# A sixteen-sequence fused layer with a hand-written order on five engines: the order of the steps is rewritten

## Chip, cores, metric

One core of one Trainium2 chip runs one program. The metric is the device time of one execution in microseconds (us), the median of several executions. TensorE (PE) multiplies, VectorE (DVE), ScalarE (ACT) and GpSimd (POOL) work element by element, SyncE (SP) issues the transfers (DMA). Each engine takes its instructions strictly in the order of its own list, and semaphores tie the lists together.

## What is computed

The input is 16 sequences of 375 rows and 128 features. Each sequence goes through three stages, and no sequence needs another one, except that the router's counts run on from one to the next.

```python
# token mixer: two-tap convolution, three gates, a scan over the rows
z, f, o = tanh(conv(x, W_z)), sigmoid(conv(x, W_f)), sigmoid(conv(x, W_o))
c = f * c + (1 - f) * z;  h = o * c
# attention over 39 fixed distances (0 to 32, 48, 64, 96, 128, 192, 256), 8 heads
q, k, v = layernorm(h) @ W_qkv
attn = softmax over the distances of (q . k[n - distance] / 4 + bias)
h = h + (attn . v[n - distance]) * sigmoid(layernorm(h) @ W_gate) @ W_out
# feed-forward with a top-2 router over 64 experts of capacity 128, one shared pair of weights
h = h + (gate of the experts that still had room) * (gelu(layernorm(h) @ w1.T) @ w2.T)
```

## The kernel before

One sequence is a chain of some 40 steps, each a small function of the program (`convolve`, `turn_x`, `project`, `score`, `turn_band`, `attend`, `up`, `down` on PE; `gelu`, `softmax_dense`, `tanh_gate` and so on on ACT). A step waits on the semaphores of the steps that it reads from and of the step that last used its buffer, issues one to 48 instructions, and adds one to its own semaphore.

The sequences are pipelined by hand. On each engine a function `turn(at)` lists the steps of one turn; `at(n)` is the sequence n places behind the newest one, and up to seven sequences are in work at once. `pipeline(engine, turn, range(...))` unrolls the turns. The first turns and the last ones are written out step by step, as lists of their own. So the order of work is nothing but the order of these lines, five times over, and an engine never takes a step ahead of one that waits.

In the text, s is the sequence whose 39 scores PE sums in the turn at hand. In the same turn s+1 is normed and projected to q, k, v and gate, s+3 and s+4 are convolved, s-1 has its attention band turned (`turn_band`), its values summed (`attend`), is turned (`turn_o`) and projected (`out_project`), and s-2 goes through the router and the feed-forward (`turn_x2`, four `up` blocks, `logits`, `positions`, `down`).

ACT uses two sets of function tables: one for tanh and gelu (called TANH in the program), one for exp and ln (LOG). The helper `table` emits a load when a step asks for the set that is not in place; copies and additions ask for none. The table in place is known only from the order of the list:

```python
            def table(name):
                if loaded[0] != name:
                    act.preload_act_table_set(name)
                    loaded[0] = name
```

The steps on ACT that matter below are: `norm2_back` (L925, copies the turned rows of s-2 for the feed-forward), `softmax_dense` (L934, exp of the 33 near scores), `softmax_far` (L941), `softmax_exp` (L950, exp of all scores), `tanh_o` (L819), `gelu` (L972), `logit_copy` (L956), `router_exp` (L965) and `tanh_gate` (L872). A table load has L799.

PE's results stand in eight PSUM banks, and each kind of result has a fixed one (`HOME`). A PE step that reuses a bank names the last users, and waits until they are read. `out_project` of s-1 (L505) shares bank 0 with the first `up` block of s-2 (L529), so it waits for `gelu(s-2, 0)`; `down` (L552) waits for gelu blocks 1 and 2.

The products of q and k are made in eight blocks of near distances and the far ones: POOL makes three of the eight and all far ones (L1724, L1709), DVE the other five (L1247). POOL's first block for a sequence waits for its q and k; `tanh_gate` of s+1 frees the bank in which the scores of s+1 begin.

Of the kernel before, what the change touches and what calls it, by code (L numbers as in the profile page):

```python
# [77 lines left out]
def build(nc, x, params, out):  # L78
# [5 lines left out]
    with ExitStack() as ctx:  # L84
# [12 lines left out]
        def P(name, a=0, b=None):  # L97
            lo, hi = COL[name]
            if lo >= PCOLS:
# [38 lines left out]
        lg = sb("lg", [128, TT, EXPERTS + 8])  # L138
# [19 lines left out]
        HOME = dict(z=4, f=1, o=7, ht=2, xb=0, q=3, k=7, v=1, g=5, s0=4, s2=5, s1=5, ts0=4, ts1=3, ts2=5, tb0=1,  # L158
                    tb1=0, tb2=6, pv=1, ot=1, op=0, x2b=4, lg=6, pos=7, up0=0, up1=5, up2=7, up3=4, dn=6)
# [99 lines left out]
        def _(sp):  # L259
# [78 lines left out]
            def turn(at):  # L338
                a0, a3, a4, a6 = at(0), at(3), at(4), at(6)
                if a4:  # L340
                    read_far(a4)
                if a0 and not (isinstance(a0.b, int) and a0.b < 3):
                    load_x(a0)
                if a4:
                    write_attn(a4)
                    read_values(a4)
                    read_band(a4)
                if a3:
                    write_values(a3)
                    read_near(a3)  # L350
                if a6:
                    store_out(a6)

            load_x(seq[3])
            write_values(seq[0])
            load_x(seq[4])
            read_near(seq[0])
            read_far(seq[0])
            write_attn(seq[0])
            read_values(seq[0])  # L360
            read_band(seq[0])
            write_values(seq[1])
            read_near(seq[1])
            pipeline(sp, turn, range(5, 17))
            read_far(seq[13])
            write_attn(seq[13])
            read_values(seq[13])
            write_values(seq[14])
            read_band(seq[13])
            read_near(seq[14])  # L370
            read_far(seq[14])
            write_attn(seq[14])
            read_values(seq[14])
            read_band(seq[14])
            write_values(seq[15])
            read_near(seq[15])
            read_far(seq[15])
            store_out(seq[11])
            write_attn(seq[15])
            read_values(seq[15])  # L380
            read_band(seq[15])
            store_out(seq[12])
# [8 lines left out]
        def _(pe):  # L391
# [164 lines left out]
            def turn(at):  # L556
                a0, a1, a2, a3, a4, a5, a6, a7 = at(0), at(1), at(2), at(3), at(4), at(5), at(6), at(7)
                if a4:
                    score(a4, 2, 0, ("s1", a4), first=True)
                    score(a4, 0, 3, last=True)  # L560
                    score(a4, 2, 1, last=True)
                if a3:
                    turn_x(a3, ("op", a6), ("up0", a7), ("tb1", a6), ("xb", a4))
                if a4:
                    turn_scores(a4, 1, ("q", a4))
                    turn_scores(a4, 0, ("s0", a4))
                    turn_scores(a4, 2, ("s2", a4))
                if a5:
                    turn_band(a5, 0, ("f", a1), ("v", a4), ("ot", a6), head=True)
                    turn_band(a5, 2, ("dn", a7), ("lg", a7), ("tb2", a6))  # L570
                if a3:
                    project(a3, "k", ("pos", a7), ("up2", a7), ("o", a2), head=True)
                    project(a3, "q", ("ts1", a4), ("q", a4))
                if a5:
                    turn_band(a5, 1, ("xb", a3), ("op", a6))
                if a6:
                    turn_x2(a6, ("ts0", a4), ("s0", a4), ("z", a1), ("up3", a7))
                if a5:
                    attend(a5, 0, ("tb0", a5), head=True)
                    attend(a5, 2)  # L580
                    attend(a5, 1)
                if a1:
                    convolve(a1, 2, ("k", a3), ("pos", a7), ("up2", a7), ("o", a2))
                if a6:
                    up(a6, 3, ("x2b", a6), head=True)
                    logits(a6, ("tb2", a5), ("dn", a7))
                if a5:
                    turn_o(a5, ("pv", a5))
                if a6:
                    up(a6, 0, ("tb1", a5), ("xb", a3), ("op", a6))  # L590
                if a0:
                    convolve(a0, 0, ("up3", a6), ("x2b", a6), ("ts0", a4), ("s0", a4), ("z", a1), head=True)
                if a6:
                    up(a6, 2, ("o", a1), ("k", a3), ("pos", a7))
                    up(a6, 1, ("ts2", a4), ("s2", a4), ("s1", a4), ("g", a4), ("up1", a7))
                if a5:
                    out_project(a5, ("up0", a6), ("tb1", a5))
                if a3:
                    value_project(a3, ("ot", a5), ("pv", a5), ("tb0", a5), ("f", a1))
                    project(a3, "g", ("up1", a6), ("ts2", a4), ("s2", a4), ("s1", a4), ("g", a4))  # L600
                if a6:
                    positions(a6, ("up2", a6))
                if a0:
                    convolve(a0, 1, ("v", a3), ("ot", a5), ("pv", a5), ("tb0", a5), ("f", a1))
                if a6:
                    down(a6, 0, ("lg", a6), head=True)
# [1345 lines left out]
```

How the kernel before makes its waits and increments, by code:

```python
        def freed(eng, users):  # L229
            for name, q_ in users:
                if q_:
                    for read in READ[name]:
                        eng.wait_ge(read, q_.b + 1)
                    return
# [1 line left out]
        def after(eng, s, n):  # L237
            if isinstance(n, int) and n <= 0:
                return
            eng.wait_ge(s, n)
# [29 lines left out]
            def write_attn(q_):  # L271
                sp.wait_ge(attn_ready, q_.b + 1)
                after(sp, band_in[q_.s], 16 * q_.g)
                for u in range(BPT):
                    rows = bass.AP(band_dram.tensor, q_.s * BAND + u * BT * BW, [[AW, BT], [128 * BW, TT], [1, SPAN]])
                    sp.dma_start(rows, attn[q_.s][u * BT:(u + 1) * BT, :, 0:SPAN]).then_inc(band_out[q_.s], 16)
# [1 line left out]
            def read_band(q_):  # L279
                sp.wait_ge(band_out[q_.s], 16 * BPT * (q_.g + 1))
                after(sp, bandT_mm[1], q_.b)
                sp.dma_start(band[:, :, :], band_rows(q_)).then_inc(band_in[q_.s], 16)
# [1 line left out]
            def write_values(q_):  # L285
                sp.wait_ge(vtok_ready, q_.b + 1)
                after(sp, v2_in[q_.s], 32 * q_.g)
                after(sp, vnear_in[q_.s], 16 * NEAR * q_.g)
                after(sp, vfar_in[q_.s], 16 * q_.g)
                rows = bass.AP(v_dram.tensor, (q_.s * (FPAD + NP) + FPAD) * D, [[D, 128], [128 * D, TT], [1, D]])
                sp.dma_start(rows, vtok[q_.s][:, :, :]).then_inc(vtok_out[q_.s], 16)
```

## Time and profile before

| what | value |
|---|---|
| time, median of 3 runs | 429.99 us (429.53 to 430.12) |
| span of the profiled execution, first to last instruction | 428.5 us |
| granted TensorE clock over the span | 0.997 of full speed |
| PE busy | 405.3 us, 95% |
| DVE busy | 380.8 us, 89% |
| POOL busy | 372.7 us, 87% |
| ACT busy | 323.1 us, 75% |
| table loads on ACT | 40, 51.3 us |
| DMA, mean busy share of 16 engines | 48.1% |

The page gives the span of the profiled execution and no time of its own for it; the median of the runs is 1.5 us longer than this span. Busy times of different engines lie beside each other, so they don't add up. The execution falls in three parts: a fill of about 75 us, in which the first sequences go through a pipeline that is not full; ten regular turns of 24.54 us each; and a drain of about 107 us, in which the turns get shorter and then empty.

### The profile page before, as it was taken

The numbers are of one execution on the slowest core, as the hardware profiler recorded it, in microseconds if no ns is written. First come the engines' busy times: TensorE is split into PE (matmuls) and PEld (weight loads), VectorE is DVE, ScalarE is ACT, GpSimd is POOL, SyncE is SP. The second block draws the span as 40 slices with busy tenths as digits, with TensorE's granted clock in tenths as the row PEclk, the third lists the DMA queues.
The fourth block names the chain that finished last, engine by engine and source line by source line (L and its number), as shares of the span: only waits on it lengthen the run. The fifth ranks groups of instructions, "written<-read, shape, count | busy, mean of one in ns | idle before, by whom it ended". The sixth has DMA issues, their size and how long they took to land.

```text
span 428.5 us, 12683 instructions
## 1 busy us (share of the span) xinstructions
PE 405.3 (95%) x4554; PEld 278.6 (65%) x4554; DVE 380.8 (89%) x873; ACT 323.1 (75%) x728; POOL 372.7 (87%) x391
## 2 busy tenths in 40 slices
PE   8788789999999999999999999999999999998884
PEld 5444364776757676776767677676767675766763
DVE  2586999899999999999999999999999999999563
ACT  3756768879687877968687887868788796859773
POOL 7696999999989989898998989898998999997611
PEclk9999999999999999999999999999999999999998
DMA  6530866462737265372826446273735547265500
GB/s 230 192 105 2 200 165 182 105 174 62 200 88 183 79 154 150 86 207 61 198 71 149 143 120 186 55 201 82 178 95 129 158 109 190 65 182 127 133 13 24
DMA packets 78702, 56.08 MB, mean 131 GB/s; under 512 B 28304, under 2 KB 71344, under 8 KB 78512
## 3 DMA queue, kind: packets, MB, share of 16 engines
q1 hardware_dynamic: 78640, 55.28, 48.1%
q8 instruction: 36, 0.59, 0.6%
q14 instruction: 26, 0.21, 0.2%
HBM read 35.56 MB, written 19.70 MB: 129 GB/s over the span
## 4 chain that ended last, share of the span: by engine, by line
PE 74%; POOL 8%; issue 3%; DVE 3%; DMA 2%; ACT 1%; SPq 0%; POOLq 0%; DVEq 0%; ACTq 0%
PE bank L456 18%; PE bank L552 9%; PE bank L529 8%; PE bank L432 6%; PE bank L405 5%; PE bank L489 5%; PE bank L406 5%; PE bank L477 4%; POOL prod L1724 4%; POOL fprod L1709 3%; PE bank L468 3%; PE bank L521 2%; PE bank L505 2%; PE bank L440 2%; PE bank L424 1%
## 5 line engine op out<-in xcount | busy, mean ns | idle before, releaser
L1724 POOL TENSOR_TENSOR prod<-q,k 128x1448 f32<-128x1448 f32 (+2 forms) x48 | 145.6, 3053 | 17.4 <-ACT k L865 13.0
L1247 DVE SCALAR_TENSOR_TENSOR prod<-bank,par,k 128x1432 f32<-128x1432 f32 (+4 forms) x80 | 134.9, 1693 | 0.0
L456 PE MATMUL bank<-prod,ew 128*32 128x374 f32 (+7 forms) x1024 | 84.3, 467 | 2.4 <-ACT gate L872 1.0
L1709 POOL TENSOR_TENSOR fprod<-q,k 128x326 f32<-128x326 f32 (+6 forms) x112 | 79.0, 742 | 0.0
L456 PEld LDWEIGHTS bank<-prod,ew 128*32 128x32 f32 x1024 | 31.4, 110 | 44.9 <-issue 37.9
L972 ACT ACTIVATE hid<-bank,par 128x374 f32<-128x374 f32 x64 | 36.3, 575 | 23.8 <-PE bank L529 22.0
L799 ACT ACT_TABLE_LOAD x40 | 51.3, 1283 | 1.4 <-PEq L1944 0.7
L529 PE MATMUL bank<-x,par 128*128 128x374 f32 x128 | 48.4, 484 | 2.0 <-ACT x L925 2.0
L552 PE MATMUL bank<-par,hid 128*128 128x128 f32 x384 | 47.9, 276 | 0.0
L552 PEld LDWEIGHTS bank<-par,hid 128*128 128x128 f32 x384 | 45.9, 192 | 2.5
L405 PE MATMUL bank<-xT,par 128*128 128x374 f32 x96 | 40.9, 508 | 1.2 <-DVE mixin L1200 0.6
L432 PE MATMUL bank<-xn,par 128*128 128x374 f32 x96 | 35.8, 482 | 4.3 <-DVE near L1294 2.5
L883 ACT ACTIVATE scT<-bank 128x374 f32<-128x374 f32 (+2 forms) x48 | 21.7, 470 | 23.1 <-PE bank L456 22.9
L406 PE MATMUL bank<-xT,par 128*128 128x374 f32 x96 | 38.0, 477 | 0.0
L1756 POOL TENSOR_TENSOR near<-near 128x384 f32<-128x384 f32 x32 | 32.4, 1013 | 1.6 <-DVE near L1294 1.6
L1756 POOL TENSOR_TENSOR near<-near,far 128x256 f32<-128x256 f32 (+1 forms) x48 | 30.9, 643 | 2.4
L529 PEld LDWEIGHTS bank<-x,par 128*128 128x128 f32 x128 | 22.4, 190 | 12.7 <-ACT x L925 2.4
L901 ACT ACTIVATE bandT<-bank 128x512 f32<-128x512 f32 (+1 forms) x48 | 26.2, 584 | 5.5 <-PE bank L477 5.5
L406 PEld LDWEIGHTS bank<-xT,par 128*128 128x128 f32 x96 | 18.4, 191 | 12.1 <-issue 0.3
L489 PE MATMUL bank<-v,bandT 128*32 128x32 f32 x1536 | 26.1, 239 | 0.0
L477 PE MATMUL bank<-par,band 128*128 128x128 f32 (+1 forms) x192 | 25.6, 270 | 0.3 <-DMA band<-band_scratch 0.3
L489 PEld LDWEIGHTS bank<-v,bandT 128*32 128x32 f32 x1536 | 23.5, 127 | 2.9 <-issue 2.8
(123 smaller groups left out, 873.6 us busy)
## 6 DMA issues: line engine op xcount, KB each, us to landing
band<-band_scratch SPq DMA_DIRECT2D x16, 768.0 KB, 5.5
band_scratch<-attn SPq DMA_DIRECT2D x64, 180.4 KB, 3.0
vnear<-v_scratch SPq DMA_DIRECT2D x48, 192.0 KB, 3.1
v<-v_scratch SPq DMA_DIRECT2D x32, 192.0 KB, 4.1
v_scratch<-vtok SPq DMA_DIRECT2D x16, 192.0 KB, 3.0
xT<-x_dram SPq DMA_DIRECT2D x16, 187.5 KB, 3.4
vfar<-v_scratch SPq DMA_DIRECT2D x16, 128.0 KB, 3.3
out_dram<-osb SPq DMA_DIRECT2D x16, 128.0 KB
```

The source lines that it names most:

```text
L405: mm(dst, P("conv", 2 * g * D, (2 * g + 1) * D), xT[q_.s][:, 0:N], start=True, stop=False)
L406: mm(dst, P("conv", (2 * g + 1) * D, (2 * g + 2) * D), xT[q_.s][:, 1:N + 1], start=False, stop=True).then_inc((z_mm, f_mm, o_mm)[g], 1)
L432: mm(home(what)[:, 0:N], weights, xn[q_.s][:, 0:N], start=True, stop=True)\
L456: done = mm(home(f"s{c}")[32 * g:32 * g + 32, lo:N], ew[:, COLS[c] + j, :], src[:, j, lo:N], start=first or only, stop=last or only)
L489: done = mm(home("pv")[BT * u:BT * (u + 1), t * D + i:(t + 1) * D:PAIRS], bandT[t][:, i * 128 + u * BT:i * 128 + (u + 1) * BT], pair, star ...
L529: mm(home(f"up{f}")[:, 0:N], P("up", f * 128, (f + 1) * 128), x2[:, 0:N], start=True, stop=True)\
L552: done = mm(home("dn")[:, t * D:(t + 1) * D], hid[:, f, t * 128:(t + 1) * 128], P("down", f * D, (f + 1) * D), start=(f == 0), stop=(f == ...
L799: act.preload_act_table_set(name)
L1247: v.scalar_tensor_tensor(bass.AP(prod[c][:, :, :].tensor, first * N + lo, [[CW * N, 128], [N, w], [1, N - lo]]), home("q")[:, lo:N].unsque ...
L1709: last = g.tensor_tensor(fprod[:, i, o:N], q[q_.s][:, o:N], k[q_.s][:, KPAD:KPAD + N - o], ALU.mult)
L1724: g.tensor_tensor(bass.AP(prod[c][:, :, :].tensor, first * N + lo, [[CW * N, 128], [N, w], [1, N - lo]]), q[q_.s][:, lo:N].unsqueeze(1).br ...
L1756: g.tensor_tensor(near[:, 0, t0:TT, :], near[:, 0, t0:TT, :], term, ALU.add).then_inc(acc_added[i], 1)
```

## The change

No step is removed or added. Both the lists of the first and last turns and the regular `turn` on PE, ACT, DVE, POOL and SP are written in another order, and the boundary between one turn and the next moves (on PE from ahead of `score(…, 2, 0)` to ahead of `attend(…, 2)`), which alone changes nothing where the cyclic order stays. Four of the PSUM homes change, k from bank 7 to 0, tb1 from 0 to 7, pos from 7 to 6 and dn from 6 to 7, and the users that the PE steps name follow. The core of the diff:

```diff
-        HOME = dict(z=4, f=1, o=7, ht=2, xb=0, q=3, k=7, v=1, g=5, s0=4, s2=5, s1=5, ts0=4, ts1=3, ts2=5, tb0=1,
-                    tb1=0, tb2=6, pv=1, ot=1, op=0, x2b=4, lg=6, pos=7, up0=0, up1=5, up2=7, up3=4, dn=6)
+        HOME = dict(z=4, f=1, o=7, ht=2, xb=0, q=3, k=0, v=1, g=5, s0=4, s2=5, s1=5, ts0=4, ts1=3, ts2=5, tb0=1,
+                    tb1=7, tb2=6, pv=1, ot=1, op=0, x2b=4, lg=6, pos=6, up0=0, up1=5, up2=7, up3=4, dn=7)
...
             # ScalarE, regular turn
                 if a5:
                     band_copy(a5, 1)
+                if a4:
+                    softmax_far(a4)
                 if a6:
                     norm2_back(a6)
                 if a4:
-                    softmax_dense(a4)
-                    softmax_far(a4)
+                    softmax_exp(a4)
                 if a1:
                     tanh_o(a1)
                 if a6:
                     gelu(a6, 3)
                     logit_copy(a6)
+                if a4:
+                    softmax_dense(a4)
+                if a6:
                     gelu(a6, 0)
                     gelu(a6, 2)
                     gelu(a6, 1)
...
             # ScalarE, first steps
             tanh_z(seq[1])
+            norm1_ln(seq[0])
             tanh_f(seq[1])
             half_forget(seq[1])
-            norm1_ln(seq[0])
             norm1_exp(seq[0])
+            tanh_o(seq[1])
             norm1_rows(seq[0])
-            tanh_o(seq[1])
...
             # TensorE, first turns: the projection of the second sequence
             convolve(seq[3], 1, ("v", seq[0]))
+            project(seq[1], "k", ("xb", seq[1]), head=True)
+            turn_h(seq[2], ("ht", seq[1]))
             score(seq[0], 1, 0, ("g", seq[0]), first=True)
...
             turn_scores(seq[0], 1, ("q", seq[0]))
             score(seq[0], 0, 3, last=True)
+            project(seq[1], "q", ("ts1", seq[0]))
```

The first place is ScalarE in a regular turn, from the copy of the last band block to the first gelu blocks (`bandT`: turned band; `x2`: rows of s-2 for the feed-forward; `ex`, `attn`: exp of the scores; `hid`: gelu). Before:

```order
L901 ACTIVATE bandT1<-bank0 128x512
L925 ACTIVATE x2<-bank4 128x374
L934 ACTIVATE attn1<-sc 128x12x33 x2
L941 ACTIVATE bank5<-sc 128x24x3
L799 ACT_TABLE_LOAD
L819 ACTIVATE bank7<-bank7,hbias 128x374
L972 ACTIVATE hid<-bank4,par 128x374
L956 ACTIVATE lg<-bank6 128x3x64
L972 ACTIVATE hid<-bank0,par 128x374
```

The same stretch of the change:

```order
L911 ACTIVATE bandT1<-bank7 128x512
L951 ACTIVATE bank5<-sc 128x24x3
L935 ACTIVATE x2<-bank4 128x374
L960 ACTIVATE ex<-sc 128x936
L809 ACT_TABLE_LOAD
L829 ACTIVATE bank7<-bank7,hbias 128x374
L982 ACTIVATE hid<-bank4,par 128x374
L966 ACTIVATE lg<-bank6 128x3x64
L809 ACT_TABLE_LOAD
L944 ACTIVATE attn0<-sc 128x12x33 x2
L809 ACT_TABLE_LOAD
L982 ACTIVATE hid<-bank0,par 128x374
```

`softmax_dense`, which needs LOG, moved from ahead of the table load to between the gelu blocks, which need TANH, and `softmax_exp` took its old place; with it come two more loads. Over the whole list ACT now has 80 loads where it had 40.

The second place is TensorE in a regular turn, from the last band block to `out_project`. Before:

```order
L477 MATMUL bank0<-par,band 128x128 x4
L513 MATMUL bank4<-par,xrow2 128x128 x2
L513 MATMUL bank4<-par,xrow2 128x118
L489 MATMUL bank1<-v20,bandT0 32x32 x16
L489 MATMUL bank1<-v20,bandT2 32x32 x16
L489 MATMUL bank1<-v20,bandT1 32x32 x16
L405 MATMUL bank7<-xT0,par 128x374
```

The same stretch of the change:

```order
L480 MATMUL bank7<-par,band 128x128 x4
L492 MATMUL bank1<-v20,bandT0 32x32 x16
L492 MATMUL bank1<-v20,bandT2 32x32 x16
L492 MATMUL bank1<-v20,bandT1 32x32 x16
L516 MATMUL bank4<-par,xrow2 128x128 x2
L516 MATMUL bank4<-par,xrow2 128x118
L408 MATMUL bank7<-xT0,par 128x374
```

`turn_x2` (`xrow2`), on whose result `norm2_back` waits, moved behind the three `attend` blocks (`v20`). From the convolution on, both lists run alike up to `out_project` and the value projection; behind that, `down` block 0 now comes ahead of the convolution, the gate projection and `positions`.

The third place is ScalarE in the drain, from the feed-forward of sequence 12 to the gate of sequence 15. In the change:

```order
L966 ACTIVATE lg<-bank6 128x3x64
L809 ACT_TABLE_LOAD
L982 ACTIVATE hid<-bank4,par 128x374
L911 ACTIVATE bandT1<-bank7 128x512
L809 ACT_TABLE_LOAD
L944 ACTIVATE attn0<-sc 128x12x33 x2
L809 ACT_TABLE_LOAD
L982 ACTIVATE hid<-bank0,par 128x374
L982 ACTIVATE hid<-bank7,par 128x374
L809 ACT_TABLE_LOAD
L960 ACTIVATE ex<-sc 128x936
L809 ACT_TABLE_LOAD
```

After this load come gelu block 1, another load, `router_exp`, the second norm of sequence 13, the value rows of 15, and one more load ahead of `tanh_gate(seq[15])`. Before, one load stood ahead of all four gelu blocks, with `tanh_gate(seq[15])` behind them.

## Rows read from the trace of the kernel before

**Rows 1.** The page, part 1: busy time of each engine, its share of the span.

```profile
PE 405.3 (95%) x4554; PEld 278.6 (65%) x4554; DVE 380.8 (89%) x873; ACT 323.1 (75%) x728; POOL 372.7 (87%) x391
```

**Rows 2.** Windows: stretch, its length, busy us of each engine, clock, DMA share, GB/s.

```profile
51.21:75.75 24.54, 22.71 (x280) 13.01 (x273) 23.29 (x39) 18.00 (x40) 24.38 (x25) 1.00 0.64 176
100.29:124.83 24.54, 24.54 (x286) 17.32 (x285) 23.45 (x55) 19.40 (x46) 24.15 (x25) 1.00 0.50 133
...
296.61:321.15 24.54, 24.54 (x286) 17.32 (x285) 23.45 (x55) 19.40 (x46) 22.39 (x23) 1.00 0.50 134
...
365.94:387.21 21.27, 21.25 (x273) 14.59 (x271) 20.37 (x46) 15.09 (x35) 21.11 (x21) 1.00 0.54 140
387.21:428.50 41.29, 30.04 (x386) 23.53 (x384) 25.32 (x92) 28.73 (x65) 16.13 (x25) 0.97 0.28 69
```

**Rows 3.** Timeline of PE in one regular turn: start, length, line, operation, tiles.

```profile
103.60 0.48 PE L513 MATMUL bank<-par,xrow 128*128 128x128 f32 x3
104.02 1.63 PE L489 MATMUL bank<-v,bandT 128*32 128x32 f32 x96
105.57 0.90 PE L405 MATMUL bank<-xT,par 128*128 128x374 f32 x2
...
111.66 0.83 PE L505 MATMUL bank<-outg,ao 128*128 128x128 f32 x6
112.32 0.83 PE L440 MATMUL bank<-par,xn 128*128 128x128 f32 x6
```

**Rows 4.** Timeline of ACT in the same turn.

```profile
104.31 0.49 ACT L925 ACTIVATE x<-bank 128x374 f32<-128x374 f32 x1
...
105.54 0.28 ACT L941 ACTIVATE bank<-sc 128x72 f32<-128x72 f32 x1
105.84 1.28 ACT L799 ACT_TABLE_LOAD   x1
107.13 0.55 ACT L819 ACTIVATE bank<-bank,hbias 128x374 f32<-128x374 f32 x1
...
109.34 0.57 ACT L972 ACTIVATE hid<-bank,par 128x374 f32<-128x374 f32 x1 [0.64 <-PE bank L529]
```

**Rows 5.** Timeline of ACT at two places of the drain without waits.

```profile
348.97 0.99 ACT L950 ACTIVATE ex<-sc 128x936 f32<-128x936 f32 x1
349.98 1.28 ACT L799 ACT_TABLE_LOAD   x1
...
372.64 0.57 ACT L972 ACTIVATE hid<-bank,par 128x374 f32<-128x374 f32 x1
373.11 0.32 ACT L956 ACTIVATE lg<-bank 128x192 f32<-128x192 f32 x1
```

**Rows 6.** All table loads: count, ns min/median/max, first and last start.

```profile
L799 ACT ACT_TABLE_LOAD  x40: 1283/1283/1283, 0.7 to 419.9; - x40
```

**Rows 7.** Timeline of POOL in the fill: near products of sequences 0, 1, 2.

```profile
22.03 9.05 POOL L1724 TENSOR_TENSOR prod<-q,k 128x1448 f32<-128x1448 f32 x3 [4.30 <-ACT q L859]
31.02 4.91 POOL L1709 TENSOR_TENSOR fprod<-q,k 128x326 f32<-128x326 f32 x7
39.44 9.06 POOL L1724 TENSOR_TENSOR prod<-q,k 128x1448 f32<-128x1448 f32 x3 [3.50 <-ACT k L865]
...
60.39 9.06 POOL L1724 TENSOR_TENSOR prod<-q,k 128x1448 f32<-128x1448 f32 x3
```

**Rows 8.** Timelines in the drain: scores of sequence 15, its gate, its softmax.

```profile
379.97 4.47 PE L456 MATMUL bank<-prod,ew 128*32 128x374 f32 x56
386.15 1.19 PE L468 MATMUL bank<-par,scT 128*128 128x128 f32 x9
...
377.18 0.58 ACT L872 ACTIVATE gate<-bank,hbias 128x374 f32<-128x374 f32 x1
...
390.36 0.97 ACT L934 ACTIVATE attn<-sc 128x396 f32<-128x396 f32 x2 [0.51 <-DVE sc L1275]
```

**Rows 9.** The page, part 6: the transfer that reads the band back, count, size, us to landing.

```profile
band<-band_scratch SPq DMA_DIRECT2D x16, 768.0 KB, 5.5
```

More of the change, by code:

```diff
@@ L574, in turn @@
+                    project(a3, "q", ("ts1", a4))
                 if a5:
[L575 to L578, printed above, removed]
+                    turn_band(a5, 1, ("dn", a7), ("o", a2))
                     attend(a5, 0, ("tb0", a5), head=True)
[L580 to L583, printed above, removed]
@@ new lines, in _ @@
+            up(seq[11], 1, ("ts2", seq[13]))
+            value_project(seq[14], ("ot", seq[12]))
+            out_project(seq[12], ("up0", seq[11]))
+            down(seq[11], 0, ("up2", seq[11]), head=True)
+            project(seq[14], "g", ("up1", seq[11]))
+            down(seq[11], 1)
+            positions(seq[11], ("lg", seq[11]))
+            turn_h(seq[15], ("ht", seq[14]))
+            down(seq[11], 2)
+            score(seq[14], 0, 1, ("up3", seq[11]), first=True)
+            score(seq[14], 1, 0, ("g", seq[14]), first=True)
@@ L723, in _ @@
             project(seq[15], "g", ("up1", seq[12]))
-            positions(seq[12], ("up2", seq[12]))
-            down(seq[12], 0, ("lg", seq[12]), head=True)
+            down(seq[12], 0, ("up2", seq[12]), head=True)
             down(seq[12], 1)
@@ new lines, in turn @@
+                if a6:
+                    attention_gate(a6)
+                if a7:
+                    route_max(a7)
+                if a2:
+                    recur_out(a2)
+                if a7:
+                    route_picks(a7)
+                if a4:
+                    products(a4, 1, 0)
+                if a6:
+                    residual(a6)
+                if a7:
+                    route_mask(a7)
+                if a4:
+                    products(a4, 0, 2)
+                if a6:
+                    stats2(a6)
@@ new lines, in turn @@
+                if a1:
+                    recur_in(a1)
+                if a7:
+                    keep(a7)
+                if a3:
+                    stats1(a3)
+                if a4:
+                    products(a4, 0, 0)
+                if a3:
+                    shift_rows(a3)
+                if a7:
+                    add_b2(a7)
+                if a4:
+                    products(a4, 0, 3)
+                if a7:
+                    take_room(a7)
+                if a6:
+                    shift2_rows(a6)
```

657 lines of the change are left out of this document (317 added, 340 removed).

## Prediction

> **What bounds the kernel now.** I read the page's busy times first: PE works 95% of the span [rows 1]. The windows by turn say where the other 5% lies: from 75.75 to 321.15 us ten turns of 24.54 us follow each other, and in nine of them PE is busy for all 24.54 us, with DVE at 23.45, POOL at 22.39 and ACT at 19.40 [rows 2]. So in the regular turns PE is the bound, without a gap. An order can't make them shorter, since the same matmuls stay; it can only open gaps. What an order could win lies in the fill (PE 22.71 of 24.54 us in the last window before the regular turns) and in the last stretch, where PE works 30.04 of 41.29 us [rows 2].
>
> **The change, regular turns.** PE's cyclic order stays but for two things: `turn_x2` moves behind the three `attend` blocks, and behind the value projection some steps swap. The bank changes keep every old waiting order or loosen it. On ACT, `softmax_dense` now stands between gelu blocks, with a table load ahead of it and one behind. A load takes 1.283 us, all 40 of them alike [rows 6], and it is not hidden: it begins at 105.84, 0.02 us after the last exp, and the next tanh begins at 107.13, 1.29 us after the load [rows 4]. Two more loads are 2.57 us of a turn in which ACT has 24.54 - 19.40 = 5.1 us free [rows 2]. By the totals they fit. What decides is where they stand.
>
> `out_project` of s-1 uses bank 0 and waits for gelu block 0 of s-2. Before, that gelu ended at 109.34 + 0.57 = 109.91, and `out_project` began at 111.66 [rows 3, 4]: 1.75 us to spare. Now I lay the new chain from the same row. The `attend` blocks take 105.57 - 104.02 = 1.55 us and `turn_x2` 0.42, so with the two swapped `turn_x2` ends at 105.57, where the convolution begins as before [rows 3]. From there on ACT has, in this order: the copy `norm2_back` 0.37 (its 0.49 less an overlap of 0.12 with what follows, an estimate), `softmax_exp` with its end 1.01 (348.97 to 349.98), load 1.29, `tanh_o` 0.47 and gelu block 3 0.47 (the spacing 372.64 to 373.11), `logit_copy` 0.34, load 1.29, `softmax_dense` 1.01, load 1.29, gelu block 0 0.57 [rows 4, 5, 8]. With 0.12 for the two hand-overs that is 8.2 us: gelu block 0 is ready at 113.8, and `out_project` is due at 111.66. **PE stands 2.1 us.** `down` block 0 then needs gelu blocks 2 and 1, 1.0 us further on ACT, but PE has `out_project` and the value projection ahead of it, twice 112.32 - 111.66 = 0.66 us [rows 3], so it adds nothing.
>
> Does the wait come back each turn? PE's way from `out_project` to the end of the next `turn_x2` is 24.54 - 6.09 = 18.45 us of matmuls without a gap, and ACT's chain starts at its end. The loop is closed: 18.45 + 8.2 = 26.7 us per turn. Nothing else can take the 2.1 us up, because PE had no gap to give. The turns with gelu blocks on ACT ahead of `softmax_dense` are those of sequences 0 to 10 in the feed-forward: ten full turns and an eleventh, the first of the drain, where one convolution (some 1.3 us, by the 0.66 us of a step half its size [rows 3]) is missing between `turn_x2` and `out_project`, so that it waits 3.4 us. Sum: 10 x 2.14 + 3.4 = **+24.8 us**.
>
> The rule that speaks against the change stands in the Trainium skill, ScalarE: Activation LUTs, Rules for kernel authors: group functions by their table set and finish one set before the next. The same page, What ACT_TABLE_LOAD costs, gives 1283 ns for the load, as here, but adds about 1380 ns for emptying the pipeline, 2.66 us per switch. The rows above show no such 1.38 us, before or behind the load; by that figure a turn would wait 4.9 us and not 2.1, and the turns would add about 55 us.
>
> **Behind PE.** With 26.7 us a turn, DVE (23.45) and POOL (22.39) have more room. DVE's `residual` waits for the late `out_project`, some 1.8 us, and POOL's `kept_mask` for `positions`, which stands 2.2 us later in PE's new order; POOL then still reaches the next near products about 1.4 us before q is ready, by adding its blocks up in the new order. Both are costed at nothing; the cover is that slack of 1.4 to 1.8 us a turn, and rival B is what happens without it. SP's transfers move too: the band of s is written after the late `softmax_dense`, 2 us ahead of `out_project`, and read a turn later. The read takes 5.5 us [rows 9]; if the write takes no longer, the band is in place 9 us behind `out_project`, and PE wants it 13.9 us behind (my count along its new list), so about 5 us remain.
>
> **Fill.** POOL's near products pace it: 9.05 + 4.91 us per sequence, and 3.50 us of waiting for k and q of sequence 1 before 39.44 [rows 7]. The new order projects both earlier, which could take that wait away (bound: -3.5 us). But ACT now has 12 loads where it had 6 before its regular turns (bound: +7.7 us). Two extra ones stand ahead of the first norm's rows (LOG, TANH, LOG, TANH around `tanh_f(1)` and `tanh_o(1)`), which puts POOL's first block at about 24.1 and not 22.03; its two blocks end at 38.0; q of sequence 1 has to wait for the turned scores of sequence 0, which need POOL's third block (33.2) and six more handovers, and comes at about 39.2. So sequence 1 starts where it did, sequence 2 at 60.4 as before, and the late `tanh_f` and gate of sequence 2 put PE 0.8 us back. I take **+0.8**, between the ends; the start of sequence 1 is the nearest row.
>
> **Drain.** Ten more loads (20 for 10), bound 0 to 12.8 us. For sequence 11 the gelu blocks are clean, but `tanh_gate(14)` stands behind a load, `router_exp` and a load: +0.8. For sequence 12 the third place in the order counts. From `logit_copy` at 370.6 (my placing; before, gelu ran at 372.64) ACT has four loads, the band copy, two exps and four gelus ahead of the end of gelu block 1, 11.0 us, then two loads, `router_exp`, the norm, the value rows and the gate of 15, 4.8 us: 386.4. Before, that gate ran at 377.18, and the scores of 15 began at 379.97 [rows 5, 8]. One of their seven near blocks (0.61 us each, a seventh of the 4.47 us less the overlap at the end) is now done earlier, six (3.7) and the far part (1.7; 386.15 - 379.97 less 4.3 and a short wait) remain: they end at 391.8, before at 386.15 [rows 8]. That is +5.7, and the softmax of 15 (390.36), its band's way through DRAM and the end hang on it. Last, sequence 14 has a load, `router_exp` and a load inside its gelus, partly hidden by the wait for the band: I take 1.0 for it. Sum **+7.5 us**.
>
> **Sum.** 428.5 + 24.8 + 0.8 + 7.5 = 461.6 us of span. The runs' median stands 1.5 us above the profiled span, so the time is **463 us**, 7.7% more.
>
> **Rivals.** A: the loads are covered, and only the fill changes. For it speak ACT's 5.1 us free a turn and the 1.75 us to spare. POOL's 3.5 us go, and the kernel is *faster*: 429.99 - 3.5 = 426.5 us (425 to 431 with the drain). It needs gelu block 0 of s-2 by 111.66, that is a chain under 6.1 us; I count 8.2, of which 2.6 are the new loads. The point from which it decides is a chain 2.1 us shorter than my sum; no row has a load that ran beside other work of ACT.
> B: the waits behind PE close a second loop. If POOL's `kept_mask`, held by `positions`, costs 1.4 us more than its slack, near products come late, scores wait, and 11 turns add another 15 us: 478. Against it: POOL and DVE each gain 2.1 us a turn.
> C: ACT stands once more behind each load, about as long as the load itself (1.28 us). Then each turn waits 2.57 us more and the drain 12.8: 463 + 11 x 2.57 + 12.8 = 504 us. Against it stand the 0.02 and 0.01 us between a load and its neighbours [rows 4]. The Trainium skill's page named above, with its 1380 ns, would have it so.
> D: the order does not do what it says. Excluded for ACT: the list has 80 loads.
>
> **Chances.** Forecast 0.83 (451 to 472), A 0.07, B 0.08, C 0.02. The forecast's own range comes from 1.6 to 2.6 us a turn (the upper end is both loads bare), which is -5.5 to +5, a fill of -2 to +3, and a drain of 3 to 12. To 8 in 10 I keep 451 to 473. A measurement tells about 0.2%, 0.9 us, from no change. Faster 0.05 and the same 0.01 come out of A; slower is 0.94.
>
> **What would show it.** In the new profile: 80 loads, 102.6 us; regular turns of 26.7 us with PE at 24.5 in them; the wait of PE ahead of the line of `out_project` released by the gelu line, about 2 us each, eleven times; ACT near 22 us a turn. POOL's first three blocks near 24.1, 39.2 and 60.4. The scores of 15 behind `tanh_gate`. Wrong would be: turns of 24.5 us (A), PE waiting in the scores for POOL's products (B), gaps of 1.4 us around the loads (C), or a fill that ends more than 3 us from where it did.

## The result, and the profile after

| | before | after |
|---|---|---|
| time, median of 4 runs | 429.80 us (429.53 to 430.12) | 477.57 us (476.98 to 478.09) |
| ratio, 95% interval | | 1.1111 (1.1095 to 1.1126) |
| span of the profiled execution | 428.5 us | 475.4 us |
| table loads on ACT | 40 | 80 |
| regular turn | 24.54 us | 26.92 us |

The forecast was 463.0 us, 451 to 473: the right side, and 14.6 us too little. The busy times and the granted clock of the changed kernel, from the page's first two parts:

```profile
PE 419.9 (88%) x4554; PEld 282.9 (59%) x4554; DVE 383.5 (81%) x873; ACT 370.6 (78%) x768; POOL 372.6 (78%) x391
...
PEclk9989899999999999999999999999998999989988
```

ACT's additional 47.5 us are the forty loads (51.3 us), less 3.8 us by which its other instructions are recorded shorter. PE has the same 4554 matmuls as in [rows 1] and is busy 14.6 us longer with them. That was in no step of the prediction; a part of it is in the 8s of the clock row. The windows, with the columns of [rows 2], a regular turn, and then the last three stretches:

```profile
120.72:147.64 26.92, 24.97 (x284) 17.06 (x284) 23.61 (x54) 21.70 (x48) 22.36 (x23) 1.00 0.46 121
...
363.05:387.20 24.15, 23.70 (x279) 17.31 (x279) 20.31 (x51) 17.04 (x42) 19.20 (x21) 0.93 0.45 124
387.20:433.00 45.80, 39.35 (x517) 27.16 (x516) 37.03 (x80) 37.26 (x73) 37.09 (x41) 0.96 0.45 122
433.00:475.40 42.40, 29.31 (x272) 22.90 (x270) 21.12 (x86) 28.17 (x61) 11.77 (x18) 0.89 0.26 64
```

A regular turn takes 26.92 us at full clock, and ACT works 21.70 us of it (19.40 before; two loads are 2.57). The forecast said 26.7. What PE waits for, in total, with the number of waits and the longest:

```profile
PE bank L508 <- ACT hid L982: 18.3, 11, 2.8
PE bank L408 <- ACT hid L982: 4.1, 10, 0.4
PE bank L435 <- ACT hid L982: 3.0, 1, 3.0
```

The first line is `out_project` (L508) behind a gelu block, eleven times: the wait that the prediction named. The second is the first convolution behind gelu block 3. The timelines of PE and ACT in one regular turn, to be held against [rows 3] and [rows 4]:

```profile
111.99 0.54 PE L516 MATMUL bank<-par,xrow 128*128 128x128 f32 x3
112.37 0.80 PE L408 MATMUL bank<-xT,par 128*128 128x374 f32 x2
...
115.21 0.80 PE L532 MATMUL bank<-x,par 128*128 128x374 f32 x2
116.41 0.87 PE L408 MATMUL bank<-xT,par 128*128 128x374 f32 x2 [0.41 <-ACT hid L982]
...
117.75 1.42 PE L532 MATMUL bank<-x,par 128*128 128x374 f32 x4
120.72 0.94 PE L508 MATMUL bank<-outg,ao 128*128 128x128 f32 x6 [1.55 <-ACT hid L982]
```

```profile
112.56 0.48 ACT L935 ACTIVATE x<-bank 128x374 f32<-128x374 f32 x1 [1.25 <-PE bank L516]
112.94 0.98 ACT L960 ACTIVATE ex<-sc 128x936 f32<-128x936 f32 x1
113.94 1.28 ACT L809 ACT_TABLE_LOAD   x1
115.23 0.55 ACT L829 ACTIVATE bank<-bank,hbias 128x374 f32<-128x374 f32 x1
...
116.51 1.28 ACT L809 ACT_TABLE_LOAD   x1
117.80 0.98 ACT L944 ACTIVATE attn<-sc 128x396 f32<-128x396 f32 x2
118.80 1.28 ACT L809 ACT_TABLE_LOAD   x1
120.09 1.50 ACT L982 ACTIVATE hid<-bank,par 128x374 f32<-128x374 f32 x3
```

`turn_x2` ends at 112.53, gelu block 0 at 120.09 + 0.57 = 120.66: a chain of 8.13 us, forecast 8.2. PE idles twice in it, 0.41 + 1.55 = 1.96 us. The other 0.43 us by which the turn is longer than 24.54 + 1.96 is in PE's busy time (24.97 for 24.54), at the same clock. The same groups in the kernel before:

```profile
108.50 0.80 PE L529 MATMUL bank<-x,par 128*128 128x374 f32 x2
109.14 0.79 PE L405 MATMUL bank<-xT,par 128*128 128x374 f32 x2
...
110.40 1.42 PE L529 MATMUL bank<-x,par 128*128 128x374 f32 x4
```

The group behind a wait is recorded longer: `out_project` 0.94 for 0.83, the convolution 0.87 for 0.79, together 0.19. The group ahead of a wait loses its overlap: the two `up` groups take 0.80 and 1.42 us in both kernels, but before, the next group began 0.64 and 1.26 us after their start (109.14 and, in [rows 3], 111.66), which makes 0.32. Some 0.10 comes back at the first convolution (0.80 for the 0.90 in [rows 3]).

The clock in the first steps, in windows of 3 us of the changed kernel:

```profile
27.00:30.00 3.00, 0.88 (x5) 0.88 (x5) 2.22 (x3) 2.99 (x8) 3.00 (x2) 0.85 0.00 0
30.00:33.00 3.00, 3.00 (x7) 1.61 (x6) 3.00 (x3) 1.13 (x3) 3.00 (x2) 0.58 0.29 86
...
48.00:51.00 3.00, 2.39 (x6) 1.35 (x6) 3.00 (x3) 2.29 (x4) 3.00 (x2) 0.77 0.65 135
51.00:54.00 3.00, 3.00 (x26) 0.88 (x28) 1.96 (x3) 2.17 (x4) 3.00 (x5) 0.67 0.98 267
```

```profile
29.15 0.86 PE L427 MATMUL bank<-par,xrow 128*128 128x128 f32 x3 [2.12 <-ACT xrow L851]
29.80 1.47 PE L408 MATMUL bank<-xT,par 128*128 128x374 f32 x2
31.07 1.45 PE L409 MATMUL bank<-xT,par 128*128 128x374 f32 x2
```

The second block is PE's timeline there. PE stands 2.12 us, and the convolutions behind it take 1.47 and 1.45 us in place of 0.80 and 0.79. A share of 0.58 is a mean over stretches at 1.00 and at 0.50, that is at the chip's two levels, 2.4 and 1.2 GHz. The other low windows of this kernel lie at 48 to 54, 363 to 369 (0.60, 0.83), 417 to 423 (0.71, 0.73), 438 to 444 (0.62, 0.81) and 456 to 462 us (0.50, 0.97), each right behind 1.7 to 3.0 us in which PE did nothing (two waits of 0.92 and 0.93 us with 0.9 us of matmuls between them at 436). The kernel before shows no window under 1.00 while it computes.

**Where the 46.9 us of span lie.** The first regular `out_project` begins at 93.79 (before 87.12): +6.7, of which 2.0 are its own wait. The eleventh begins at 363.05 (before 331.26): +31.8, so ten turns of growth are +25.1. The rest, +15.1, is the drain.

### The profile page after: what moved, and what is told of

Same layout as the page of the kernel before. It is cut to its first block, busy times and chain, and to the rows that moved or that the text cites. A ratio compares the mean times of both kernels' runs of the same rounds, so it can differ in the third digit from the quotient of the medians.

```text
span 475.4 us, 12735 instructions
## 1 busy us (share of the span) xinstructions
PE 419.9 (88%) x4554; PEld 282.9 (59%) x4554; DVE 383.5 (81%) x873; ACT 370.6 (78%) x768; POOL 372.6 (78%) x391
## 4 chain that ended last, share of the span: by engine, by line
PE 59%; ACT 22%; issue 11%; DVE 4%; DMA 1%; SPq 1%; ACTq 0%; POOLq 0%; DVEq 0%; POOL 0%
PE bank L459 19%; ACT L809 11%; PE bank L555 8%; PE bank L435 6%; PE bank L492 4%; PE bank L480 4%; ACT hid L982 4%; PE bank L471 3%; PE bank L408 2%; PE bank L409 2%; ACT ex L960 2%; PE bank L508 2%; PE bank L443 2%; DMA band<-band_scratch 1%; ACT attn L944 1%
## 5 line engine op out<-in xcount | busy, mean ns | idle before, releaser
L809 ACT ACT_TABLE_LOAD x80 | 102.6, 1283 | 2.1 <-PEq L1968 0.7
L555 PE MATMUL bank<-par,hid 128*128 128x128 f32 x384 | 53.2, 294 | 2.8 <-ACT hid L982 2.8
L555 PEld LDWEIGHTS bank<-par,hid 128*128 128x128 f32 x384 | 50.6, 210 | 3.5 <-ACT hid L982 3.0
L1787 POOL TENSOR_TENSOR kept<-kept,msk 128x192 f32<-128x192 f32 x16 | 8.8, 550 | 36.7 <-DVE kept L1391 36.7
L982 ACT ACTIVATE hid<-bank,par 128x374 f32<-128x374 f32 x64 | 33.2, 573 | 0.6 <-PE bank L532 0.4
L508 PE MATMUL bank<-outg,ao 128*128 128x128 f32 x96 | 15.3, 297 | 19.4 <-ACT hid L982 18.3
L508 PEld LDWEIGHTS bank<-outg,ao 128*128 128x128 f32 x96 | 12.2, 194 | 28.2 <-ACT hid L982 27.6
L492 PE MATMUL bank<-v,bandT 128*32 128x32 f32 x1536 | 26.7, 238 | 1.0 <-ACT bandT L911 1.0
```

The source lines that it names most:

```text
L555: done = mm(home("dn")[:, t * D:(t + 1) * D], hid[:, f, t * 128:(t + 1) * 128], P("down", f * D, (f + 1) * D), start=(f == 0), stop=(f == ...
L982: A(hid[:, f, 0:N], home(f"up{f}")[:, 0:N], ACT.Gelu, bias=bias(B1 + f)).then_inc(gelu_ready[f], 1)
```

## The experiments

The kernel before ran beside each of the three groups of experiments, with medians of 429.55, 430.24 and 429.57 us; the changed kernel ran only in the first comparison (before: 429.80), so differences to its 477.57 us carry up to half a us of that.

**Undoing ScalarE's three places.** All four start from the changed kernel and put steps of ACT back; the other engines keep the new order. a_reg, the regular turn:

```diff
                 if a6:
                     logit_copy(a6)
-                if a4:
-                    softmax_dense(a4)
-                if a6:
                     gelu(a6, 0)
...
                 if a4:
                     softmax_far(a4)
+                    softmax_dense(a4)
```

> The changed kernel with one step put back: in ScalarE's regular turn softmax_dense stands behind softmax_far, ahead of the table load, as before the change (56 loads instead of 80; all lists of first and last turns unchanged). If the two loads in ScalarE's chain from turn_x2 to gelu block 0 make the turns long, the regular turns fall from 26.9 to 24.5 us and the time by 27 us, to 450 us. If the new order of the other four engines makes them long (PE behind POOL or DVE), the turns stay above 25.5 us and the time above 462 us.

Measured: 452.82 us (452.65 to 453.54), 56 loads, -24.75 us. The wait of `out_project` for a gelu block is gone from the list, the one of the convolution (4.1 us in ten times) stays, and the turn takes 25.10 us. That is short of what I had expected (24.5 us and 450 us): the other wait had been left out. One step of ACT carries over half of the loss.

a_fill puts `norm1_ln` of sequences 0 and 2 back behind the tanhs of the first steps (four loads fewer); a_drain puts the gates and gelus of the last sequences ahead of `router_exp` and the exps (ten fewer). The core of a_drain:

```diff
+            tanh_gate(seq[14])
             router_exp(seq[11])
-            tanh_gate(seq[14])
...
             gelu(seq[12], 2)
-            softmax_exp(seq[14])
             gelu(seq[12], 1)
-            router_exp(seq[12])
...
             tanh_gate(seq[15])
+            router_exp(seq[12])
...
+            softmax_exp(seq[14])
```

> The changed kernel with four table loads less in ScalarE's first steps (norm1_ln(0) behind half_forget(1), tanh_o(1) behind keep_rows(0), tanh_o(3) ahead of norm1_ln(2)). If the loads late in the chain of the first norm put the fill back, sequence 1 starts on POOL 2 us earlier than at 41.3, and the time falls by 3 to 5 us, to about 473.5 us. If POOL's own blocks and the wait for the turned scores pace the fill, the time moves by less than 1 us.

> The changed kernel with ten table loads less in ScalarE's last steps (gelu blocks of sequences 12 and 14 kept together, tanh_gate of 14 and 15 ahead of router_exp). If the loads hold PE there, the last 15 us of loss fall to about 5 and the time to about 467.5 us. If the drain is long for another reason (the order of PE, DVE or the band's transfers), the time stays above 474 us.

> All three edits together: the new order on PE, VectorE, GpSimd and SyncE, ScalarE with 42 loads. If the three losses add up, 477.6 - 27 - 4 - 10 = 436.5 us. If the new order of the other engines is better than the old one and only the loads hid it, under 429 us. If the order of the other engines costs by itself, 440 us or more.

Measured: a_fill 476.33 us (474.91 to 476.59), -1.2; a_drain 467.35 us (465.69 to 467.53), -10.2; all three together, a_all, 443.72 us (443.55 to 444.07), ratio 1.0323 (1.0307 to 1.0339), with 42 loads. The drain came as expected. The fill did not: taking out its four loads gave a third of what I had expected. In the profile of a_fill the first `out_project` comes 1.8 us earlier (91.98 for 93.79) and the end 0.6, but the clock stayed at 1.00 from 48 to 54 us there, and in the drain it was low in other places (360 to 369, 444 to 450), so this run doesn't part the loads from the clock. And with almost as few loads as before, 14.2 us were still missing. So "twice the loads" was not the whole cause. The expectation laid a result above 440 us to the order of the other engines; a later run (a_exp, below) shows that nearly half of the 14.2 us was still ACT's order.

**Is it the place of the step, or the number of loads?** Two edits of the kernel before. b_dense moves nothing but `softmax_dense` to the changed kernel's place (64 loads):

```diff
                 if a4:
-                    softmax_dense(a4)
                     softmax_far(a4)
...
                     logit_copy(a6)
+                if a4:
+                    softmax_dense(a4)
+                if a6:
                     gelu(a6, 0)
```

> The kernel before, whole, with one step of ScalarE's regular turn moved: softmax_dense from ahead of softmax_far to between logit_copy and gelu block 0, as the change has it (two table loads more in each of 11 turns, 64 in all; every other engine as before). My theory (the position of the exponential between turn_x2 and gelu block 0 makes the loss of the regular turns): gelu block 0 is ready at about 112.9 us of the turn of rows 3, where out_project stood at 111.66, so TensorE waits some 1.2 us in each of 11 turns and its next matmuls are lengthened by about 0.3: +13 to +18 us, 443 to 448 us. Rival (the loss of the changed kernel's turns needs the other engines' new order as well): under +3 us, below 433. Rival (every table load costs its 1.28 us wherever it stands): 22 x 1.28 = +28 us, 458.

b_loads moves nothing and puts two loads there, which change the table to LOG and back (62 loads in all):

```diff
                     logit_copy(a6)
+                    table(LOG)
                     gelu(a6, 0)
```

> The kernel before with two table loads more ahead of gelu block 0 in each of 11 regular turns and no step moved (64 loads in all, as many as the run with softmax_dense moved). My theory: in the turn of rows 4 ScalarE stands 0.64 + 1.31 us in this place, so 2.57 us of loads put gelu block 0 at 111.28 to 111.85 where out_project needs it at 111.66: a wait of 0.2 us a turn and a little lengthening, +2 to +5 us, 432 to 435 us. Rival (each load costs its time on the way to the end): 22 x 1.28 = +28 us, 458 us. Rival (fully hidden): within 0.5 us of 429.6.

Measured: b_dense 446.66 us (445.39 to 448.27), +16.4; b_loads 434.62 us (434.18 to 435.22), +4.4. ACT loads its table 24 times more than before in b_dense and 22 times more in b_loads (62 loads in all, not the 64 of the expectation): the other two of b_dense lie in the first turn, where no gelu follows. Timelines of ACT in b_loads and of PE in b_dense:

```profile
108.81 2.57 ACT L799 ACT_TABLE_LOAD   x2
111.39 1.50 ACT L972 ACTIVATE hid<-bank,par 128x374 f32<-128x374 f32 x3
```

```profile
112.21 1.42 PE L529 MATMUL bank<-x,par 128*128 128x374 f32 x4
114.75 0.94 PE L505 MATMUL bank<-outg,ao 128*128 128x128 f32 x6 [1.11 <-ACT hid L972]
```

In b_loads the two loads fill the 1.95 us in which ACT stood here before, gelu block 0 is ready at 111.96, and `out_project` begins at 112.02: the turn grows by 0.38 us. With the exp between the loads (b_dense) the chain is 1 us longer still, and PE stands 1.11 us each turn. Two loads cost 0.4 us a turn or 1.4, by what they push past the moment at which PE comes for the result; 1.28 us each (+28 us) would be wrong by a factor of six for b_loads.

**Is it the chain from turn_x2?** a_x2first is the changed kernel with `turn_x2` 1.03 us earlier on PE, all 80 loads kept:

```diff
+                if a7:
+                    turn_x2(a7, ("ts0", a5))
                 if a6:
                     attend(a6, 2)
                     attend(a6, 1)
-                if a7:
-                    turn_x2(a7, ("ts0", a5))
```

> The changed kernel, whole, with one step of TensorE's regular turn moved: turn_x2 ahead of the two attend steps instead of behind them, 1.03 us earlier; all 80 table loads stay. My theory (PE waits because the chain turn_x2 to gelu block 0 on ScalarE takes longer than TensorE's own work between them): the start of the chain comes 1.0 us earlier in each of 11 turns, the wait ahead of out_project falls from 1.55 to some 0.5 us: 11 x 1.0 = -11 us, 465 to 468 us. Rival (ScalarE as a whole is too slow for the turn, or waits for something else than turn_x2 at that place, as its own steps ahead of it): within 2 us of 477.6.

Measured: 466.72 us (466.36 to 467.35), -10.9, and the wait list says the same:

```profile
PE bank L508 <- ACT hid L982: 13.5, 11, 2.4
```

The turn fell from 26.92 to 26.15. ACT's list is the same, with its 80 loads; only the start of the chain moved. The total came as expected, the parts did not. The turn fell by 0.77 us and not by 1.03: the 0.41 us ahead of the convolution are gone, but the wait ahead of `out_project` only fell from 1.55 to 1.12, since the chain from the end of `turn_x2` to `out_project` took 8.38 us for 8.19. Of the 11.0 us of span that it gained, 7.8 lie between the first and the eleventh `out_project`, 1.9 ahead of them, where the clock now stayed at 1.00 from 27 to 33 us, and 1.3 behind them. That these add up to 11 was luck. The loop PE, `turn_x2`, ACT, gelu block 0, PE sets the turn.

**The clock.** a_standin is the changed kernel with matmuls that nobody uses, into a bank that is free at the time, in PE's two long waits of the first steps:

```diff
             def turn_x(q_, *before):
                 freed(pe, before)
+                if q_.b == 1:
+                    stand_in(3)
                 pe.wait_ge(xrow_ready, q_.b + 1)
...
+                if q_.b == 1 and what == "g":
+                    stand_in(3)
                 freed(pe, before)
```

> The changed kernel, whole, with three stand-in matmuls (128 x 374, the shape of a convolution, into a bank that nothing uses yet) in each of TensorE's two long waits of the first steps: ahead of turn_x of sequence 1 (2.12 us idle at 27.0) and ahead of the gate projection of sequence 1 (2.65 us at 45.9). Theory (the granted clock falls to its lower level behind those idle stretches because the engine stood idle): the windows 27 to 33 and 48 to 54 us show 1.00 in place of 0.85, 0.58, 0.77 and 0.67, which gives back 3 x (0.15 + 0.42 + 0.23 + 0.33) = 3.4 us of matmul time, less what the stand-ins take beyond the idle time (under 0.5): 474 to 475.5 us. Rival (the clock falls there for another reason, or the time is hidden by a wait that comes later): the windows stay low, or they are full and the time stays within 1 us of 477.6.

Measured: 474.12 us (473.23 to 474.80), -3.45. Windows and PE's timeline of this run:

```profile
27.00:30.00 3.00, 2.86 (x11) 1.56 (x10) 2.22 (x3) 2.99 (x8) 3.00 (x2) 1.00 0.00 0
30.00:33.00 3.00, 3.00 (x21) 1.48 (x23) 3.00 (x3) 1.43 (x4) 3.00 (x2) 1.00 0.28 86
```

```profile
27.04 2.05 PE L424 MATMUL bank<-par 128*128 128x374 f32 x6
29.22 0.54 PE L433 MATMUL bank<-par,xrow 128*128 128x128 f32 x3
29.60 0.90 PE L408 MATMUL bank<-xT,par 128*128 128x374 f32 x2
```

`turn_x` of sequence 1 starts at the same place (29.22 for 29.15), but the clock stays at 1.00 and the convolution behind it takes 0.90 us, not 1.47. More work made the kernel faster. How much of the 3.45 us is the stand-ins' own? The first `out_project` begins 2.1 us earlier (91.68 for 93.79), and so does the eleventh (360.93 for 363.05). The other 1.2 of the 3.3 us of span come behind it, where nothing was changed: this profile has the low clock in two places of the drain (360 to 366 and 408 to 414), the changed kernel's has it in four. So 2.1 us are shown, and that the total met the expected 3.4 was luck. POOL shows where this went on: its blocks for sequences 1 and 2 began at

```profile
41.33 9.06 POOL L1745 TENSOR_TENSOR prod<-q,k 128x1448 f32<-128x1448 f32 x3 [3.73 <-ACT k L875]
...
63.01 6.07 POOL L1745 TENSOR_TENSOR prod<-q,k 128x1448 f32<-128x1448 f32 x2 [1.66 <-ACT k L875]
```

in the changed kernel, and with the stand-ins at

```profile
40.24 9.04 POOL L1753 TENSOR_TENSOR prod<-q,k 128x1448 f32<-128x1448 f32 x3 [2.45 <-ACT k L883]
...
60.90 6.05 POOL L1753 TENSOR_TENSOR prod<-q,k 128x1448 f32<-128x1448 f32 x2 [0.68 <-issue]
```

**The missing 14 us.** The first of three runs from a_all adds stand-ins in the fill as above and in the drain (one ahead of `turn_x2` and of the first `up` of sequences 14 and 15, one ahead of `out_project` of 14, two ahead of `turn_band` of 15). The second moves one more step of ACT's regular turn:

```diff
                 if a6:
                     norm2_back(a6)
-                if a4:
-                    softmax_exp(a4)
                 if a1:
                     tanh_o(a1)
...
                 if a5:
                     norm2_exp(a5)
+                if a4:
+                    softmax_exp(a4)
```

> The run with all three undoings (443.7 us, 14.2 over the kernel before) with stand-in matmuls in TensorE's idle stretches of the first steps (3 ahead of turn_x of sequence 1, 3 ahead of the gate projection of sequence 1) and of the last ones (1 ahead of turn_x2 and 1 ahead of the first up of each of sequences 14 and 15, 1 ahead of out_project of 14, 2 ahead of turn_band of 15). In that run the granted clock stood low in 27 to 33 (0.81, 0.62), 411 to 420 (0.53, 0.50, 0.83) and 426 to 432 us (0.87, 0.56): 1.7 + 3.4 + 1.7 = 6.8 us of matmul time. Theory (the clock falls behind idle stretches, and that is about half of what is left): 1.00 in all of them, and 4 to 6 us regained, since a part of the last steps waits for ScalarE anyway: 438 to 440 us. Rival (the rest is waits of the new order, the clock is hidden by them): within 1.5 us of 443.7.

> The run with all three undoings with one more step of ScalarE's regular turn put back: softmax_exp from ahead of tanh_o and gelu block 3 to the end of the turn. There TensorE waits 0.41 us for gelu block 3 ahead of a convolution in 10 turns, and its turn takes 25.10 us, where the kernel before takes 24.54. Theory (1.0 us of softmax_exp stands on the path from turn_x2 to gelu block 3): that wait goes, the turn takes 24.5 to 24.6 us, -5 to -6 us, 437.5 to 439 us. Rival (another engine's order holds the turn at 25.1, or GpSimd and VectorE, which use what softmax_exp writes, wait for it now): within 1.5 us of 443.7 or above it.

> The same (all undoings, softmax_exp at the end of the turn) with the same stand-in matmuls. Theory: the two gains add, 432.5 to 435 us, which leaves 3 to 5 us over the kernel before for the order of the other four engines. Rival (they overlap): at or above the lower of the two others, 437 or more.

| kernel | loads | regular turn | time | ratio to before (95%) |
|---|---|---|---|---|
| a_all | 42 | 25.10 | 443.72 | 1.031 to 1.034 |
| a_all_si | 42 | 25.10 | 440.23 (439.83 to 440.35) | 1.023 to 1.027 |
| a_exp | 42 | 24.45 | 437.13 (435.73 to 437.70) | 1.015 to 1.019 |
| a_exp_si | 42 | 24.45 | 434.15 (432.98 to 435.38) | 1.008 to 1.014 |

The second came 0.4 us below its expected range, the third within it; the stand-ins alone brought 3.5 us, under the 4 to 6 expected: the windows were at 1.00 everywhere while PE computed, and 6.8 us of matmul time gave back half of that at the end, 0.7 us of it by the first `out_project` (88.36 for 89.10). A regular turn with `softmax_exp` at its end, in windows:

```profile
113.68:138.13 24.45, 24.45 (x285) 17.18 (x284) 23.42 (x55) 19.35 (x46) 22.38 (x23) 1.00 0.51 134
```

PE has no gap, and the turn is 0.09 us shorter than before. So the new order of PE, DVE, POOL and SP costs nothing in the regular turns. `softmax_exp` stood between `norm2_back` and gelu block 3 and cost 6.6 us, with not one load more or less (42 in both). The profiled run of a_exp_si was one of its two shorter ones (433.31 us; the median is 4.6 us over the kernel before). Of the 2.6 us of span that it has over the kernel before, 0.9 are there at the first `out_project` (88.03 for 87.12), none at the eleventh (331.31 for 331.26), since its turns are shorter, 0.3 at the last one (409.74 for 409.41), and 2.3 come behind it; I did not take them apart. No version beat the kernel before.

## Why the prediction was right and wrong

The forecast was 461.6 us of span, and 475.4 were measured. Of the 13.8 us between them 3.9 lie in the fill, 2.4 in the turns and 7.6 in the drain (the first turn's own wait was 0.1 less than forecast). The steps that failed are the terms of the fill and of the drain, and the granted clock that all terms took as 1.00.

**The bound, and the wait of `out_project`: right.** PE bounds the kernel, an order can only open gaps in it, and the gap came where the forecast put it, eleven times. The chain took 8.13 us (8.2 forecast). b_dense, b_loads and a_x2first show that this chain, and not ACT's total or the count of loads, decides.

**The term of a turn: right mechanism, a little small.** Forecast 2.14 us, measured 2.38. The idle time was even less, 1.96; the 0.43 us that it lacked are the matmul groups around a wait, the one ahead of it without its overlap and the one behind it longer. I had taken PE's time between the waits as unchanged (18.45 us). From the first to the eleventh `out_project` the forecast had 9 x 2.14 + 3.4 = 22.7 us more than before, and 25.1 were measured, though the eleventh wait was 2.78 us and not 3.4.

**The fill, +0.8: this step failed.** It measured +4.7 beside the first turn's own wait. POOL's first block was forecast at 24.1 and came at 23.71; the next two were forecast at 39.2 and 60.4 and came at 41.33 and 63.01. My chain of handovers used matmul durations of full clock. With the clock held (a_standin), 40.24 and 60.90 come out, and 2.1 us of the 4.7 are gone. With the four loads of the fill undone as well, a_exp_si has 0.9 left at the same place. So, as an estimate from these two, 1.7 us are the loads and the steps moved with them, and 0.9 the order of the other engines. The term of 0.8 had neither the clock nor the loads at their size.

**The drain, +7.5: mis-sized by half, +15.1.** Its place was right: a_drain, which undoes ACT's order there, gave 10.2 back; the low clock of 417 to 423, 438 to 444 and 456 to 462 us went with it, so its share is in that number. The gate of 15 comes at 421.31; forecast was 386.4, plus the 31.8 us by which the drain began later, 418.2. From `logit_copy` to this gate ACT took 15.8 us (405.51 to 421.31), exactly the 11.0 + 4.8 forecast; it began 3.1 us later than I had placed it. Sequences 11 and 14 were put at +0.8 and +1.0. By the starts of `turn_x` of 15 (+35.3 in all), of the last turned scores (+41.4) and of the end (+46.9) the three parts are +3.5, +6.1 and +5.5: the middle one, which I worked out step by step (+5.7), is nearly right, and the two that I took by feel are not.

Other traces take these two apart. Behind the eleventh wait the changed kernel needs 24.15 us to the next `out_project` at a clock of 0.93; a_reg, with the same PE list and no wait there, needs 22.61 at 1.00, so the low clock is about 1.5 of the 3.5 us. (b_dense and b_loads, with one PE list, agree: 22.75 us at 0.92 and 21.09 at 1.00.) The kernel before needs 21.35: another 1.3 belong to the new order of the engines, and only the last 0.7 to the stretch with the wait for `tanh_gate(14)`, which was the forecast's 0.8. Behind the last `out_project` the changed kernel takes 23.40 us, and a_standin, a_fill and a_x2first, with the same lists from there on, 22.45 to 22.54 with the clock at 1.00: 0.9 of the 5.5 us is the clock. 2.3 us behind that `out_project` stay in a_exp_si too, and their cause is open.

ACT's timeline shows how sequence 12 came about:

```profile
412.88 1.28 ACT L809 ACT_TABLE_LOAD   x1
414.17 0.98 ACT L960 ACTIVATE ex<-sc 128x936 f32<-128x936 f32 x1
415.17 1.28 ACT L809 ACT_TABLE_LOAD   x1
416.46 0.57 ACT L982 ACTIVATE hid<-bank,par 128x374 f32<-128x374 f32 x1
417.06 1.28 ACT L809 ACT_TABLE_LOAD   x1
...
421.31 0.57 ACT L882 ACTIVATE gate<-bank,hbias 128x374 f32<-128x374 f32 x1
```

On PE the same place is an idle stretch with the low clock behind it: 24 matmuls of `down` take 4.47 us, and such a group takes 2.92 us at full clock in a_exp_si.

```profile
417.09 0.90 PE L435 MATMUL bank<-xn,par 128*128 128x374 f32 x2 [3.04 <-ACT hid L982]
417.82 4.47 PE L555 MATMUL bank<-par,hid 128*128 128x128 f32 x24
```

**The clock: in no term.** This is the term that was left out, not mis-sized. The granted clock stood at 1.00 in every row that I had read of the computing part, and I carried it over to a kernel with other idle stretches. Of PE's 14.6 us of additional busy time, 10 x 0.43 and the eleventh are 4.7 us in the regular turns; the other 10 lie in the first and last steps, where the low windows are. What of these reached the end was shown for the fill (2.1 us), in the drain for the two stretches above (1.5 and 0.9 us), and, with the loads undone, for fill and drain together (3.5 and 3.0 us). For the low clock at 417 to 423 us it stays open: no profile has the stretch around it at 1.00 throughout with ACT's list as changed.

**The rivals.** A (the loads are covered) fell: it wanted a chain 2.1 us shorter. B (a second loop behind PE) would have given 478, 0.4 us from the result, and is wrong all the same: the turn was 26.92 us and not 28, and a_exp shows that POOL and DVE in their new order hold nothing. A time that fits is no proof of its mechanism. C (1.28 us more at each load) fell by the timeline: from the end of the instruction ahead to the load, and from the load's end to the next instruction, it is 0.01 to 0.03 us, as in [rows 4]; only the first load has a wait for PE behind it. The Trainium skill (ScalarE: Activation LUTs, What ACT_TABLE_LOAD costs) has about 1380 ns of draining with each switch; its 1283 ns for the load agree with all 80 here, the draining is in none of them. The rule of the Trainium skill (same page, Rules for kernel authors) to group functions by table set holds in this case where a result is waited for; b_loads paid 0.2 us for each load, most of which stood in free time.

## What to carry to other kernels

Work out an order change on the engine that is not the bound as a loop: from the step of the bound engine that starts the chain to the step that needs its result; count everything that now stands in between, cheap exps as well as loads. An instruction inside that chain costs up to its whole length each turn (the exp of 1.0 us cost 0.65); the same exp at the end of the turn cost nothing. Where a change opens idle stretches of 2 us and more on TensorE, put a term for the clock behind each of them; and take the parts of a drain as carefully as a regular turn, since little there is covered: ten loads (12.8 us) and the steps moved with them cost 10.2.

## What the hardware did that I had not expected

TensorE's clock fell to its lower level behind idle stretches of 2.1 to 3.0 us inside a kernel that is busy for 88% of its span, in one place behind 1.70 us. The wait of 1.55 us in each regular turn was never followed by it. Nor does it fall every time behind the same wait: the 24 matmuls of `down` of sequence 14, in the changed kernel and in a_standin, which runs the same lists there:

```profile
456.04 4.42 PE L555 MATMUL bank<-par,hid 128*128 128x128 f32 x24 [1.70 <-ACT hid L982]
```

```profile
453.58 2.92 PE L563 MATMUL bank<-par,hid 128*128 128x128 f32 x24 [1.68 <-ACT hid L990]
```

So it is with the wait ahead of the gate projection of sequence 1, in the windows of the kernel before and of b_dense, whose first 40 us run through the same steps on PE:

```profile
45.00:48.00 3.00, 3.00 (x21) 1.46 (x23) 3.00 (x3) 1.58 (x4) 3.00 (x2) 1.00 0.95 232
```

```profile
45.00:48.00 3.00, 3.00 (x7) 2.01 (x8) 3.00 (x2) 1.09 (x3) 3.00 (x2) 0.50 0.95 230
```

PE stood 2.51 us in the one (clock 1.00 behind it) and 2.50 in the other (0.50). In the profiles taken here this place kept the clock in the kernel before, in b_loads, a_fill, a_drain, a_all and a_exp, and lost it in the changed kernel, a_reg, b_dense and a_x2first. The four runs of b_dense are spread over 2.9 us, those of the kernel before in the first comparison over 0.6; that the clock makes this spread was not shown, and two of those four runs have the same mean clock, 0.993, and lie 2.4 us apart. The Trainium skill (TensorE: Matmul & The Clock Gate, HAM oscillation) tells of matmul kernels that fall back to the lower clock in waits for transfers; here the waits were for other engines, and the trace agrees that the lower clock follows a wait (0.71 and 0.73 behind the 3.04 us at 417).

A wait cost PE more than its idle time, at a granted clock of 1.00: the group behind it took 0.08 to 0.11 us longer than the same group without a wait (0.87 for 0.79, 0.94 for 0.83), and the group ahead of it lost 0.16 us of overlap with the next. With two waits a turn this was a fifth of what the turn lost (0.43 of 2.38 us).
